# Sorting the edges of a GNN layer: tables of the buckets on 49 partitions, 16-bit lookups, and a swapped sort product

## The reference

```
messages = x[src] * edge_weight[:, None]
agg = segment_sum(messages, dst, 6250)
h = relu(((x + agg) @ W1 + b1)) @ W2 + b2          # gnn, hidden 512
k, v = ln(x per head), ln(x per head)               # mix, 8 heads of 32
kv = k^T v / N per block of 256 nodes;  mix = x @ kv + x
topk_vals, topk_idx = top_k(gate(.), 2)             # ffn, 16 experts of 512
out = layernorm(sum of two experts + residual) * gamma + beta
```

## Time and profile before

| | before |
|---|---|
| three runs, us | 2083.77, 2087.97, 2088.9 |
| profiled execution, its own time | 2086.33 us |
| its span | 2084.2 us |
| busy: PE, DVE, ACT, POOL | 87%, 68%, 36%, 58% |
| first matrices of stage 4 start | 161.80 us |
| last sort product ends | 405.44 us |
| mean granted TensorE clock | 0.94 of 2.4 GHz |

### The profile page before, as it was taken

The page is one execution under the profiler, slowest core; times in us unless marked ns, Lnnn a source line. Parts: engine busy times, 40 slices in busy tenths (PEclk is TensorE's granted clock), DMA queues, the critical chain, the costliest instruction groups (busy, mean ns, idle before and its releaser), DMA issues. The chain is left out here.

```text
span 2084.2 us, 43884 instructions
## 1 busy us (share of the span) xinstructions
PE 1814.0 (87%) x12300; PEld 1634.0 (78%) x12300; DVE 1411.1 (68%) x4015; ACT 741.2 (36%) x2167; POOL 1206.1 (58%) x1244
## 2 busy tenths in 40 slices
PE   6306999758889999999999999999977999999986
PEld 4206889657878888888888888878766999999974
DVE  5899788758996777677767776657554555555547
ACT  5806778500101333333333332222222333333347
POOL 1003444477777777777777777777703555555424
PEclk9657999979999999999999999999978999999999
DMA  5000101054444444444444444444425642222248
GB/s 174 0 0 21 39 22 39 22 166 149 137 132 120 129 127 129 130 134 129 128 129 128 130 125 125 123 121 128 120 84 163 208 126 72 72 72 72 69 148 316
DMA packets 130018, 232.33 MB, mean 111 GB/s; under 512 B 25990, under 2 KB 82616, under 8 KB 129703
## 3 DMA queue, kind: packets, MB, share of 16 engines
q0 software_dynamic: 56096, 144.39, 23.8%
q1 hardware_dynamic: 46039, 59.76, 8.8%
q10 hardware_dynamic: 27696, 25.83, 3.9%
HBM read 187.46 MB, written 42.43 MB: 110 GB/s over the span
## 5 line engine op out<-in xcount | busy, mean ns | idle before, releaser
L1337 POOL DMA_INDIRECT lower<-xn_rows,lower x858 | 826.9, 964 | 261.5 <-issue 232.8
L1502 DVE TENSOR_SCALAR lower<-bank,lower 128x128 f32<-128x128 f32 x960 | 347.1, 404 | 69.6 <-issue 53.1
L1362 PE MATMUL bank<-ones,ident 128*128 128x128 f32 x2376 | 322.5, 278 | 23.3 <-DVE xh L1519 17.8
L1362 PEld LDWEIGHTS bank<-ones,ident 128*128 128x128 f32 x2376 | 307.4, 192 | 40.4 <-DVE xh L1519 20.7
L1378 PE MATMUL bank<-lower 128*128 x960 | 292.2, 386 | 19.9 <-SPq L1207 13.1
L1519 DVE TENSOR_TENSOR xh<-xh,bank 128x256 f32 x480 | 199.3, 415 | 158.4 <-PE bank L1379 156.9
L1379 PE MATMUL bank<-lower 128*128 x960 | 287.3, 380 | 0.0
L608 POOL DMA_INDIRECT edge_records_sorted<-lower x112 | 113.2, 1011 | 292.3 <-ACT lower L771 266.7
L2003 DVE TENSOR_SCALAR arena<-bank,b_tile 128x128 f32<-128x128 f32 x456 | 128.4, 345 | 166.4 <-PE bank L1881 166.4
L1881 PEld LDWEIGHTS bank<-arena 128*128 128x128 f32 x1824 | 224.6, 194 | 14.6 <-ACT arena L1936 8.9
L1881 PE MATMUL bank<-arena 128*128 128x128 f32 x1824 | 225.6, 278 | 8.1 <-ACT arena L1936 8.1
(11 more groups left out here) (347 smaller groups left out, 2594.7 us busy)
## 6 DMA issues: line engine op xcount, KB each, us to landing
lower<-xn_rows,lower POOLq DMA_INDIRECT x858
lower<-in_L_ffn_w SPq DMA_DIRECT2D x16, 512.0 KB
upper<-in_L_ffn_w SPq DMA_DIRECT2D x16, 512.0 KB
xn_rows<-xh SPq DMA_DIRECT2D x7, 896.0 KB, 4.1
lower<-xn_rows ACTq DMA_DIRECT2D x49, 128.0 KB
xn_rows<-lower ACTq DMA_DIRECT2D x49, 128.0 KB
x_plus_beta<-lower ACTq DMA_DIRECT2D x49, 128.0 KB
upper<-in_x SPq DMA_DIRECT2D x1, 6144.0 KB
```

Of the source, the lines that this page charges most:

```text
L1337: pool.indirect_dma_start(edge_rows[:, t % ROUND, :], None, xn_dram, bass.IndirectOffsetOnAxis(source.bitcast(U32)[:, t:t + 1], 0)).then_i ...
L1362: pe.matmul(sums_at(u)[:, 0:P], ident[:], ones[:], start=True, stop=True)
L1502: dve.tensor_scalar(edge_sel[:, (2 * u + h) % ESEL, :], iota_gather, lane[:, at:at + 1], weight_s[:, at:at + 1], ALU.is_equal, ALU.mult).t ...
```

## The change

It has four parts.

1. *Counts earlier.* `count(r)` stands behind every second distance. `upto_b` has ones in its column 0 and counts strictly before a partition elsewhere, so that row 0 of the result holds totals and the others hold the counts that the lookups need. One DMA on SP turns the 49 x 28 totals from that row onto 49 partitions.
2. *Tables small.* With buckets on partitions, each table is 49 partitions x 28 and each step a small operation (new L828 to L866). TensorE gives the sums over buckets and copies onto all partitions with small products (`sums(d)`, new L652 to L666), placed behind distances 16, 17, 19 and 21. The wide products L675, L676, the one-column products L683 and the three wide operations of `bucket_order` are gone. Three copies and three small operations more stand ahead of the rounds.
3. *Lookups in 16 bits.* `start` and `pos` are unsigned 16-bit, the columns lie by column and then group, so the innermost dimension of 28 is contiguous in all operands. The mask compares `bkt_c` (the same layout).
4. *Sort product swapped.* The one-hot of the rows (128x128) is the stationary operand and the values (128x64) are the moving one; the result is already 128x64. The transpose, the first of the two copies and their waits are gone. The address product has a bf16 operand of 114 partitions.

Beside that, `ranks` of stage 5 moves from bank 5 to bank 3, up to two units later or earlier in the schedule, and its wait moves from `second` to `turn`.

```diff
-            pe.matmul(bank[2 + p][:, c:c + 1], past_m[p][0:NT + 1, c * P:(c + 1) * P], ones[0:NT + 1, 0:1], ...)
+            pe.matmul(bank[2 + p][:, c:c + 1], past_m[p][0:KB, c * P:(c + 1) * P], steps_b[0:KB, ds(g, 1)], ...)
...
                 for e in range(GC):
-                    mm = pe.matmul(bank[6 + p][0:NQ * QW, 0:P], moving[p][:, e].rearrange("p c w -> p (c w)"),
-                                   row_hot[p][:, e, :], start=e == 0, stop=e == GC - 1)
+                    mm = pe.matmul(bank[6 + p][:, 0:NQ * QW], row_hot[p][:, e, :], moving[p][:, e].rearrange("p c w -> p (c w)"),
+                                   start=e == 0, stop=e == GC - 1)
                 mm.then_inc(s_qmm, 1)
-                pe.wait_ge(s_qx, g + 1)
-                pe.sem_inc(s_apart, 1)
-                pe.transpose(bank[1][:, p * P:p * P + NQ * QW], quads_across,
-                             ident[0:NQ * QW, 0:NQ * QW]).then_inc(s_qT, 1)
...
                 act.wait_ge(s_qmm, 2 * g + 2)
-                act.activation(quads_across, bank[6 + p][0:NQ * QW, 0:P], ACT.Copy).then_inc(s_qx, 1)
-                act.wait_ge(s_qT, g + 1)
...
-                act.activation(quads[i], bank[1][:, p * P:p * P + NQ * QW], ACT.Copy).then_inc(s_qcp, 1)
+                act.activation(quads[i], bank[6 + p][:, 0:NQ * QW], ACT.Copy).then_inc(s_qcp, 1)
...
-                if d % 4 == 3:
-                    count(d // 4)
+                if d % 2 == 0 and d <= 2 * NR:
+                    count(d // 2 - 1)
+                sums(d)
...
+            sp.wait_ge(s_cnt, NR)
+            sp.dma_start(totals[0:NT, :], cnt[0:1, :]).then_inc(s_totals, 16)
...
+            dve.tensor_tensor(bg(spread)[kb], ident[kb, 0:NT].unsqueeze(2).to_broadcast([NT, NT, NGRP]),
+                              bucket_fq8[kb, :].unsqueeze(1).to_broadcast([NT, NT, NGRP]), ALU.mult).then_inc(s_small, 1)
...
+                dve.scalar_tensor_tensor(start[:, at], cnt[:, at], not_first, bank[2 * c][:, 0:nb * NGRP], ALU.mult, ALU.add)
...
-                    dve.tensor_scalar(masks[b % 4], bkt_f, iota_n[:, b:b + 1], None, ALU.is_equal).then_inc(s_dve, 1)
+                    dve.tensor_scalar(masks[b % 4], bkt_c, iota_n[:, b:b + 1], None, ALU.is_equal).then_inc(s_dve, 1)
...
-                    dve.copy_predicated(bg2(pos), bg2(masks[(b - 1) % 4]), start[:, (b - 1) * NGRP:b * NGRP].unsqueeze(2)
-                                        .to_broadcast([P, NGRP, GC])).then_inc(s_dve, 1)
+                    dve.copy_predicated(columns(pos), columns(masks[(b - 1) % 4]), start[:, (b - 1) * NGRP:b * NGRP].unsqueeze(1)
+                                        .to_broadcast([P, GC, NGRP])).then_inc(s_dve, 1)
...
             def bucket_order():
-                dve.tensor_tensor(by_bucket, iota_n[:, 0:NT].unsqueeze(2).to_broadcast([P, NT, NT]),
-                                  bucket_rank.unsqueeze(1).to_broadcast([P, NT, NT]), ALU.is_equal).then_inc(s_dve, 1)
...
-            while any(u + d - T_SECOND in turn_unit for d in (-1, 0, 1)):
+            while u in turn_unit or u - 1 in turn_unit:
                 u += 1
...
-        gate_at, ranks_at = bank[6][:, D:D + NX], bank[5][:, D:D + NX]
+        gate_at, ranks_at = bank[6][:, D:D + NX], bank[3][:, 0:NX]
```

More of the change, by code:

```diff
@@ L203, in gps_layer @@
         carve = carver(xh, NT * D)
-        start = carve(NBG)
-        sort_at = NBG
+        start = carve(NBG // 2).bitcast(U16)
+        sort_at = NBG // 2
+        assert NBG % 2 == 0 and QE * ((GC * P + NT * (QE - 1)) // QE) + GC * P < 1 << 16
         carve = carver(xh[:, sort_at:NT * D], NT * D - sort_at)
@@ L659, in edges_tensor, with sums @@
                 pe.matmul(bank[6 + h][:, 0:EH], minus_b, bkt_c[:, cols], start=False, stop=False)
+            def sums(d):
+                if d == 16:
+                    pe.wait_ge(s_clear, 4)
+                    pe.wait_ge(s_consts, 7)
+                    pe.wait_ge(s_small, 1)
+                    pe.matmul(first_at, before[0:NT, 0:NT + 1], quads_b[0:NT, :], start=True, stop=True).then_inc(s_pref, 1)
+                if d == 17:
+                    pe.wait_ge(s_small, 2)
+                    pe.matmul(keys_at, key_wide[0:NT, :], ident[0:NT, 0:NT], start=True, stop=True).then_inc(s_pref, 1)
+                    pe.wait_ge(s_small, 3)
+                    for c, (b0, nb) in enumerate(BANKS):
+                        pe.matmul(bank[2 * c][:, 0:nb * NGRP], ones[0:NT, :], spread[0:NT, b0 * NGRP:(b0 + nb) * NGRP],
+                                  start=True, stop=True).then_inc(s_pref, 1)
+                if d == 19:
+                    pe.wait_ge(s_small, 4)
+                    pe.matmul(bases_at, ahead[0:NT, :], total_one[0:NT, :], start=True, stop=True).then_inc(s_pref, 1)
+                if d == 21:
+                    pe.wait_ge(s_small, 5)
+                    pe.matmul(sorted_at, key_wide[0:NT, :], placed_at[0:NT, :], start=True, stop=True).then_inc(s_pref, 1)
+                    pe.matmul(steps_at, one_less[0:NT + 1, 0:NT + 1], due_b[0:NT + 1, :], start=True, stop=True).then_inc(s_pref, 1)
             differences(1)
@@ L665, in edges_tensor @@
                     differences(d + 2)
-                if d % 4 == 3:
-                    count(d // 4)
[L668 to L684, removed]
+                if d % 2 == 0 and d <= 2 * NR:
+                    count(d // 2 - 1)
+                sums(d)
+            assert 2 * NR < 16 and 16 * NGRP >= EH
             def sort(r, i):
@@ L793, in edges_vector @@
             n = dve_n
+            high, low = slice(0, NT + 1), slice(LOW, KB)
             dve.memset(src_i, 0).then_inc(s_clear, 1)
@@ new lines, in edges_vector @@
+            dve.memset(first_col, 0.0).then_inc(s_dve, 1)
+            dve.memset(steps_b, 0.0).then_inc(s_dve, 1)
+            dve.tensor_tensor(one_less, ident[:], shift_down, ALU.subtract).then_inc(s_dve, 1)
+            dve.tensor_scalar(not_first, iota_pc[:, 0:1], 1.0, None, ALU.min).then_inc(s_dve, 1)
+            n.add(7)
+            dve.wait_ge(s_totals, 16)
+            then(dve.tensor_scalar(totals_i[kb, :], totals[kb, :], float(QE - 1), None, ALU.add))
+            then(dve.tensor_scalar(totals_i[kb, :], totals_i[kb, :], QSHIFT, None, ALU.arith_shift_right))
@@ L914, in edges_vector @@
                 cols = slice(h * GC // 2, (h + 1) * GC // 2)
[L915 removed]
+                dve.tensor_tensor(by_column(pos_i)[:, cols, :], columns(pos)[:, cols, :],
                                   bank[6 + h][:, 0:EH].rearrange("p (j g) -> p j g", g=NGRP), ALU.add).then_inc(s_dve, 1)
```

200 lines of the change are left out of this document (85 added, 115 removed).

## The result

The changed kernel takes 2156.79 us, the median of 4 runs (2155.64 to 2158.72), against 2088.39 before (4 runs): a ratio of 1.0334, 95% interval 1.0316 to 1.0351. Slower by 68 us, where 2150 with a range of 2125 to 2180 was forecast. Its profiled execution takes 2158.72 us, 72.4 more than that of before, with a span of 2157.0.

What follows compares the result with a forecast made beforehand. The prediction took VectorE alone to bound the kernel between counts and rounds, and TensorE in the rounds. Its terms summed as 2086.33 - 45.6 + 110.2 - 0.7 = 2150 us, with a range of 2125 to 2180.

Steps and rivals of the forecast that it cites:

- Counts and tables: Before the lookups: they start at 57.3 us instead of 93.58, 36.3 us saved, between 33 and 40.
- Lookups: 49 masks and predicated copies on VectorE: a pair takes 1.05 us instead of 1.25, 9.8 us saved, ends 0 and 20.
- Unpacking: Between lookups and rounds: 6.6 us as before plus 0.8, first matrices at 116.2 us instead of 161.80, 45.6 earlier.
- Rounds: 28 groups of the sort product at 12.4 us each, 347.2 us against 237.0 before, 110.2 us more.
- The step with the most doubt: In the rounds: TensorE's clock stays at 1.2 GHz to their end, a product takes 11.95 us.
- Later stages: Stage 5, where the ranks move in the schedule: 0 us, ends -3 and +3.
- the shorter way to the scatter: End of the rounds: the last product reaches the scatter over one copy, 0.7 us saved.
- the large term: The rounds' loss from the swapped sort product at the low clock: 110.2 us more.
- B: Rival for the rounds: busy TensorE raises the clock, a group takes 6.8 us at most, 1995 us in all; chance 0.11.
- C: Rival for the rounds: full clock but loads not hidden, a group takes 9.7 us, 2075 us in all; chance 0.03.
- D: Rival for the rounds: low clock and loads not hidden, a group takes 18.4 us, 2318 us in all; chance 0.02.
- E: Rival for the rounds: the clock rises now and then, for half of the groups, 2072 us in all; chance 0.04.

Runs made afterwards that it cites:

- e8: The changed kernel with 128 moving columns in the sort product (second 64 of the result unused) and the ranks as before: 1998.81 us, ratio 0.9574.
- e3: The changed kernel with 128 moving columns instead of 64 in each matmul of the sort product but the last: 2307.50 us on another chip, ratio 0.9667.
- e4: The changed kernel with 46 f32 128x128 matmuls into an unused bank before the first sort product: 2431.15 us on another chip, ratio 1.0206.
- e10: The changed kernel with 46 full matmuls as warm start and 6 full f32 matmuls ahead of each later sort product: 2038.71 us, ratio 0.9754.

## Why the prediction was right, point by point

*Counts and tables.* Forecast 57.3 for the start of the lookups, measured 55.78. The copy of the last counts ends at 42.86 and not 45.4, the DMA took 2.4 us as taken (42.86 to 45.22), the chain 10.6 us for 9.4: the spread products of 49 partitions take 4.94 us on TensorE in three pieces, for which each of the three copies waits.

*Lookups.* The mis-sized term: a pair takes 1.22 us, not 1.05, 1.6 us saved and not 9.8. I had put the value in the middle between no gain and the ratio of the mask's operation; the end of no gain was nearly right. By the Trainium skill (page "Vector Engine (DVE) Microarchitecture Reference", section "5.1 Performance modes — why throughput varies by op and dtype") predicated copy is not among the operations with two results a cycle, and this trace agrees: 960 ns for 784 elements of 16 bits, where the mask, a tensor_scalar operation of 16 bits, takes 410.

*Unpacking.* 7.4 us forecast, 7.44 measured. First matrices at 123.27 for 116.2: 7.1 late, all of it the lookups less what the tables gave.

*Rounds.* The step with the most doubt, that the clock would not rise, held: the clock stayed at 0.50 through every group. The product was forecast at 11.95 us and takes 12.0 to the start of the addresses behind it (129.88 to 141.88). The four addresses take 0.15 us and not 0.45: their operand is bf16, and I had priced them by the f32 row. So the rounds take 339.8 us for 347.2, 7.4 less.

*Later stages.* Taken as 0 with ends of 3 us, measured 9 us in the profile (72.4 less 64.2, and the 0.7 of the shorter way to the scatter on top) and 7.5 to 16 in the experiments. Stage 5 alone loses 15.6 us; the way from the last product to its first sum is 3.6 us shorter where 0.7 was forecast, and the way to the experts 2.5. This is the other mis-sized term, and its range of 3 us either way was too narrow. I had read the small waits at the ranks of before as a price for any place; but the edit adds a wait for ScalarE's copy of rows turned two units earlier, and TensorE, busy 1030 of 1080 us in that stage before (440 to 1520), stands some 0.9 us at 17 of the 49 ranks:

```profile
1021.08 0.17 PE L1374 MATMUL bank<-lower,upper 128*128 128x16 bf16 x1 [0.87 <-ACT lower L1235]
```

Asking which copy the new wait is for, and how late it ends, would have found it.

*The sum.* Errors of +7.1, -7.4 and about +9 leave +8.7 on the profiled execution (2158.7 for 2150). That two of them cancel is luck; the large term, 110 us forecast and 102.8 measured (339.8 less 237.0), is not. The range does not come out of its own terms either: they give 2150 less 17 and plus 22 at most, 2133 to 2172, and not 2128 to 2175.

*The rivals.* B is right about what the rounds are once the clock is up (e8), and wrong about what raises it: TensorE was busy by both counts throughout and stayed at 1.2 GHz. The Trainium skill (page "TensorE: Matmul & The Clock Gate", section "Part 1: The HAM clock gate (the "warmup" mystery)") says that the gate goes by how busy TensorE has been recently; read so that a load counts as busy it does not agree with this trace, 340 us busy at 0.50, nor with e3, in which only streamed columns were added. C and D fall by e4 and by the trace after: 6.42 us at 2.4 GHz and 11.98 at 1.2 leave no room for a stream behind each load. E did not occur in the changed kernel.

## What to carry to other kernels

Which operand of a product is stationary and which moves does not only set the columns to load and to stream: where loads are the longer side, TensorE looks fully busy and can still be left at half its clock. When an engine's busy share is near 1 and every instruction takes twice its time, read the granted clock before looking for a wait, and try a wider stream, even of columns that are thrown away. A pause can cost the clock for the work behind it (in the kernel before, 5.36 us idle and then a group of 11.54 us for 7.98), so a change that removes such a pause can be worth more than the pause.

## What the runs showed of the hardware that was not expected

Twice the moving columns with the same loads made a product faster, 6.44 us for 12.2. After a warm start the narrow stream held 2.4 GHz over two products and lost it in the third (e4); 12 full matmul instructions a group, which also left no idle time, kept it to the end (e10). In the kernel before, with the wide stream, the clock fell twice for some 3 us (near 243.7 and 277.9), each time in the product behind 2.06 us without one (240.53 to 242.59, 274.52 to 276.57); three later stretches of that length, in the three groups of 8.4 us, did not cost it, and no run shows why. With the clock at 0.50, four products with loads of 128 bf16 columns start within 0.15 us, some 37 ns each, and those with loads of 128 f32 columns 214 ns apart. And the same program takes 14% longer on another chip, most of it in stage 5.
